# Heads and the turn of h ahead of a round of scores, and turned scores ahead of the queries

## The reference

```python
q, k, v = x @ wq.T, x @ wk.T, x @ wv.T            # 16 heads of q, 4 of k and v
attn = softmax(where(causal, q @ k / sqrt(16), -inf))
h = c + (attn @ v) @ wo.T
w, sel = top_k(rmsnorm(h) @ gate_w.T, 2)
```

## Time and profile before

| | us |
|---|---|
| median of 3 runs | 2118.55 |
| lowest, highest | 2116.47, 2120.29 |
| profiled execution | 2111.37 |
| its span | 2109.7 |
| TensorE busy | 2036.1 (97%) |
| VectorE busy | 1347.3 (64%) |
| ScalarE busy | 1117.4 (53%) |
| GpSimd busy | 963.0 (46%) |

### The profile page before, as it was taken

The page is one execution under the profiler, slowest core; times in us unless marked ns, Lnnn a source line. Parts: engine busy times, 40 slices in busy tenths (PEclk is TensorE's granted clock), DMA queues, the critical chain, the costliest instruction groups (busy, mean ns, idle before and its releaser), DMA issues. The chain is left out here.

```text
span 2109.7 us, 50236 instructions
## 1 busy us (share of the span) xinstructions
PE 2036.1 (97%) x17544; PEld 1752.2 (83%) x17544; DVE 1347.3 (64%) x2818; ACT 1117.4 (53%) x2219; POOL 963.0 (46%) x1062
## 2 busy tenths in 40 slices
PE   7999989999999999989979999999899999999997
PEld 7999985666666666659979999999888888888886
DVE  7888954676777767765636776788654444444452
ACT  6777744666666666655543333344354444454542
POOL 0000002365565556556644444444245656565653
PEclk9999987999999999989989999999999999999998
DMA  8767711133233232229864444544344444545442
GB/s 294 264 260 267 261 59 31 62 104 96 92 108 110 87 106 96 78 92 305 300 218 144 148 151 142 175 150 151 104 96 109 95 111 95 112 96 111 96 83 30
DMA packets 134682, 289.62 MB, mean 137 GB/s; under 512 B 23026, under 2 KB 64755, under 8 KB 128243
## 3 DMA queue, kind: packets, MB, share of 16 engines
q1 hardware_dynamic: 84466, 177.25, 24.9%
q0 software_dynamic: 50048, 110.14, 20.3%
HBM read 187.17 MB, written 95.42 MB: 134 GB/s over the span
## 5 line engine op out<-in xcount | busy, mean ns | idle before, releaser
L1248 DVE TENSOR_REDUCE neg_max<-ring 128x2 f32<-128x512 f32 (+1 forms) x384 | 250.0, 681 | 106.4 <-PE ring L1734 106.1
L1041 POOL TENSOR_SCALAR_AFFINE_SELECT weights_diag<-weights_diag 128x512 f32<-128x512 f32 x256 | 158.3, 643 | 258.4 <-ACT weights_diag L1139 258.1
L2908 POOL DMA_INDIRECT out<-q_t,row_put x128 | 201.8, 1576 | 162.4 <-ACT q_t L2972 137.7
L3046 DVE TENSOR_TENSOR ex_hid<-ex_up_ps,gelu 128x512 f32<-128x512 f32 x128 | 86.9, 688 | 171.8 <-ACT gelu L2956 171.8
L2956 ACT ACTIVATE gelu<-ex_gate_ps 128x512 f32<-128x512 f32 x128 | 76.3, 596 | 187.3 <-PE ex_up_ps L62 187.3
L2379 POOL DMA_INDIRECT picked_rows<-results,lo_row_now x128 | 134.0, 1047 | 56.3 <-issue 29.8
L1139 ACT ACTIVATE weights_diag<-ring 128x512 f32<-128x512 f32 x256 | 138.5, 599 | 24.2 <-PE ring L1752 24.2
L60 PE MATMUL ex_down_ps<-ex_dn_lo,ex_hid_hi 128*128 128x256 f32 x512 | 145.1, 283 | 2.8 <-issue 2.8
L61 PE MATMUL ex_down_ps<-ex_dn_hi,ex_hid_lo 128*128 128x256 f32 x512 | 145.2, 284 | 0.0
L62 PE MATMUL ex_down_ps<-ex_dn_hi,ex_hid_hi 128*128 128x256 f32 x512 | 144.9, 283 | 0.0
L1049 POOL DMA_INDIRECT sorted_rows<-h_sb,row_now x128 | 126.8, 990 | 34.8 <-issue 31.3
(11 more groups left out here) (404 smaller groups left out, 7521.8 us busy)
## 6 DMA issues: line engine op xcount, KB each, us to landing
ug_raw<-in_w_ug SPq DMA_DIRECT2D x32, 1028.0 KB, 5.0
dn_raw<-in_w_dn SPq DMA_DIRECT2D x32, 640.0 KB, 5.2
q_t<-sorted_rows SPq DMA_DIRECT2D x136, 128.0 KB
moe_w<-in_expert_gu SPq DMA_DIRECT2D x16, 1024.0 KB, 4.8
results<-c0n POOLq DMA_DIRECT2D x33, 256.0 KB, 4.4
x_raw<-in_x_t SPq DMA_DIRECT2D x32, 256.0 KB, 5.1
c0n<-c SPq DMA_DIRECT2D x32, 256.0 KB, 4.3
c0r<-c SPq DMA_DIRECT2D x32, 256.0 KB
```

The lines of the kernel that those rows point to most:

```text
L1041: nc.gpsimd.affine_select(part, part, [[0, G], [1, P]], ALU.is_ge, 0.0, base=0, channel_multiplier=-1).then_inc(kept_done, 1)
L1248: nc.vector.tensor_reduce(out, src, AX_X, ALU.max, negate=True).then_inc(max_done, 1)
L2908: nc.gpsimd.indirect_dma_start(out=out_rows, out_offset=bass.IndirectOffsetOnAxis(ap=at, axis=0), in_=eo[c][:, n, :], in_offset=None, comp ...
L3046: nc.vector.tensor_tensor(hid[f % 2][:], up_ps[f % 2][:], gelu[f % 2][:], ALU.mult).then_inc(hid_done, 1)
```

## The change

TensorE: heads q0 comes ahead of the turn of h, heads q1 ahead of S1, and T2 ahead of the first half of the queries. VectorE: the first maximum of S1 comes behind the reciprocal and the quotients of q1. ScalarE: the third and fourth exponent of T0 come ahead of the square sums of batch i+3, and those behind `norm_high`. No instruction is added or removed, and no wait is: each waits for what it waited for before, in its new place.

```diff
@@ ScalarE, body(i)
                 if has:
                     exps(i, 0, (0, 1))
-                if exists(later(i, 3)):
-                    front.square_sums(act, i[1] + 3)
-                if has:
                     exps(i, 0, (2, 3))
                 if has_next:
                     front.norm_high(act, i[1] + 2)
+                if exists(later(i, 3)):
+                    front.square_sums(act, i[1] + 3)
                 if has_before:
                     empty_values(i, 1)
@@ VectorE, body(i)
                     divide(i, 0)
                 if has_h:
                     h_low(i)
-                if has_scores:
-                    maxima(s, 1, 0)
                 if has_before:
                     inverse_sums(i, 1)
                 if picks:
...
                 if has_before:
                     divide(i, 1)
                 if has_scores:
+                    maxima(s, 1, 0)
                     maxima(s, 1, 1)
@@ TensorE, body(i)
                 if has:
                     turned_scores(i, 1)
+                if has_before:
+                    heads(i, 0)
                 if has_h:
                     turn_h(i)
                 if has_before:
-                    heads(i, 0)
+                    heads(i, 1)
                 if has_scores:
                     scores(i, 1)
-                if has_before:
-                    heads(i, 1)
                 if has_next:
                     keys_values(i)
-                    queries(i, 0)
                 if has:
                     turned_scores(i, 2)
+                if has_next:
+                    queries(i, 0)
```

## The result

| | before | after |
|---|---|---|
| median of the comparison | 2119.26 | **2136.30** |
| lowest, highest (4 runs each) | 2116.47, 2120.29 | 2132.94, 2138.62 |
| ratio, 95% interval | | 1.0081, 1.0063 to 1.0100 |
| profiled execution | 2111.37 | 2138.62 |
| its span | 2109.7 | 2137.0 |

The change costs 17 us, 0.8%; forecast were 21.4 us and 2140. The profiled spans differ by more, 27.3 us, since the profiled execution of before was 5 us under its fastest timed one, and that of after was its slowest. By the starts of T0 the 27.3 us split as follows: up to step 2 -3.5; steps 2 to 29 +20.0 (544.66 to 564.66); step 30 +1.6; from T0 of step 31 through layer 0's experts +3.9, and through the next stage +5.3. Apart from step 31 the last two lie outside the edits. TensorE spent 28.6 instead of 14.2 us of the one, and 15.8 instead of 10.5 of the other, at a granted clock of 0.5.

The account below looks back on a forecast made before the run. TensorE, busy for 97% of the span, was taken as the bound. 16 batches x 0.47 = 7.5, 13 x 0.97 = 12.6 and ends +1.3 gave +21.4 us on 2118.55, so 2140 us; range 2129 to 2149.

Parts of the forecast that it names:

- T2's wait: In batches with picks, T2 waits for S1's maxima behind a late `chosen`: +0.50 us in each of thirteen.
- Heads q1 waits for VectorE: Heads q1, now ahead of S1, waits 0.53 us for VectorE's quotients: +0.58 us per batch.
- S1's hidden wait: Inside S1, key groups 2 and 3 wait for T1's exponents; starting later removes this: -0.19 us per batch.
- Switches around T2: T2 ahead of the queries changes passes to row-tiled products: 0 to 0.1 us, taken as +0.08 per batch.
- ScalarE's copy taken at nothing: Values copy ahead of heads q0: square sums of 0.96 us fit in its 1.36 us of waiting, costing nothing.
- rival 1: `chosen` slips in between two of GpSimd's selects and T2 is not held up: 2133.5 us; chance 0.22.
- Ends: First and last batches: batch 30 +1.5 us, batch 31 -0.2, batches -1 and 0 nothing; together +1.3 us.
- rival 2: Two idle gaps in each even batch halve TensorE's clock: 32 us on top, 2172 us; chance 0.07.

Follow-up runs that it names:

- e12: The changed kernel a third time, nothing altered, timed beside the kernel before: 2122.59 us, ratio 1.0047.
- e1: The kernel before with only the heads order of TensorE and VectorE changed: 2128.75 us, ratio 1.0075.
- e7: The changed kernel with the turn of h ahead of both heads rounds: 2136.37 us, ratio 1.0100 to the kernel before.
- e2: The kernel before with only T2 put ahead of the first half of the queries: 2123.62 us, ratio 1.0040.
- e10: The kernel before with T2 ahead of the first queries everywhere and `chosen` moved behind S1's second maximum: 2112.82 us, ratio 0.9990.
- e5: The kernel before with the changed heads order and T2 ahead of the first queries, ScalarE's order as before: 2126.92 us, ratio 1.0055.
- e3: The kernel before with only ScalarE's order changed: 2111.37 us, ratio 0.9994.
- e8: The changed kernel once more, nothing altered, timed beside the kernel before: 2124.15 us, ratio 1.0045.
- e4: The changed kernel with heads q1 back behind S1 and VectorE's first maximum back ahead of q1's reciprocal: 2117.13 us, ratio 1.0012 to the kernel before.
- e9: The kernel before with T2 ahead of the first queries only in steps without picks: 2107.70 us, ratio 0.9972.
- e11: The kernel of e10 with ScalarE's order changed too: 2110.84 us, ratio 0.9980 to the kernel before.

## Why the prediction was right, and where it was not

The number was near, 2140 against 2136.3, and inside the range. That is in part luck. The mechanism behind most of it was right, but one term (T2's wait, 6.5 us) did not occur, the start of the stage gained what I had put at nothing, and an execution with late counts, which I had not forecast, filled the gap. In the two other comparisons the same change cost less than half of the forecast.

- **Heads q1 waits for VectorE: right.** In e12 heads q1 starts 665.93 - 663.39 = 2.54 us after T1, and the forecast was 664.45 - 661.91 = 2.54. The waits show it about once in each step, e1 has it alone, e7 lengthens the step by 0.44, which is what the turn covered.
- **S1's hidden wait goes: right**, 1.35 us. Together with the wait I had 0.39 us a step; e1 measured 0.45 and 0.47. What the other 0.06 to 0.08 are stays open.
- **Switches around T2, +0.08: wrong in sign in odd steps.** e2 has -0.07 there. In even ones the kernels with the new place take 0.04 to 0.05 more (e10, e5); what of this is the place is not shown. As a sum over the steps that is about -0.5 us instead of +2.3.
- **ScalarE's copy taken at nothing: right** by e3, e8 and e12. Late copies there were in the first comparison, but ScalarE was idle before them in all steps but step 10. There the square sums did hold the copy, once late high parts had used up the cover.
- **T2 held up in even steps, +0.50 each, 6.5 us: wrong.** The step that failed is "So I take that `chosen` ends at 647.52 as before". It ended at the next joint of two selects, and rival 1 describes that: no T2 waits for the maxima in steps 4 to 28 of e12 or of the changed kernel. The row for `gap` misled me, and it was not the nearest: in each trace `gap` took 1.55 us in step 30 alone and 0.10 to 0.16 in all others. For `chosen` the rows of before said as much: it started at 646.90, at the joint of the third and fourth select (645.09 + 1.79 = 646.88), so its 0.62 us were one select as well. In step 26 of before it came just at that joint and took 0.13. The rule of the Trainium skill (SBUF — State Buffer, section "Who interferes with whom"), by which the one that starts first keeps the ports for its whole instruction, was the better guide: `chosen` waited for one instruction at most in all these traces (0.61, 0.32). `gap`, at 1.55 us through two joints, does not fit it in the traces of before and after.
- **Ends, +1.3: near for step 30, but blind to the start.** Step 30 took 1.6 us more in two of the three traces of the change and 2.5 in e12 (forecast +1.5). I had counted batches -1 and 0 at nothing. With T2 ahead, step 0 takes 24.0 to 24.6 us, and without it 25.2 to 26.3, in all traces. In e8 T0 of step 2 comes at 359.0 instead of 363.3, so -4.3 us, at less half clock. Of these 3.3 lie ahead of step 0. T0 of step 0 starts at 314.6 to 315.8 in seven of the eight traces with ScalarE's new order (317.8 in e7) and at 317.1 to 318.4 in the six without it. So that order probably gives some 3 us at the start; in e3, which has it alone, longer steps 0 and 1 took most of that back.
- **The clock, rival 2:** no half clock in the middle of the stage in the change, with a gap of some 0.4 us in every step. Such stretches came in e2 and e4, where T2 waits, but in e10 too, where nothing does; so what decides them stays open.

The sum for e8, by its trace: -4.3 before step 2, +12.75 in steps 2 to 29, +1.6 in step 30, -0.8 behind it, 9.2 us (spans 2118.9 and 2109.7). That is the price of the change in two of three comparisons, and my 21.4 are more than twice that. Rival 1's 14.9 us come closer: its 0.47 in each of 28 steps are 13.2, against 12.75. In the first comparison the same kernel had the late counts on top. Its span is 18.1 us above that of e8, and 564.66 - 557.41 = 7.3 of these lie between steps 2 and 30. Another 4.1 and 5.9 lie in the two stretches behind, with 14.6 and 5.7 us more at half clock. So late copies can account for the 7.3 and not for the whole. That all four executions of the first comparison were disturbed alike is what their times suggest; only one was profiled.

Open is why TensorE's counts came late in that execution. ScalarE's order, the heads order and T2's place, alone or in the pairs tried, don't bring it, nor does the whole kernel in e8 and e12, and it reaches into a stage where nothing was changed. So it most likely belongs to the execution or to its chip, and which of them is not shown: e8 and e12 ran on two different chips, and which one ran the first comparison isn't on record.

## What to carry to other kernels

Before two rounds are put next to each other that use one bank in turn, take the other engine's answer from the trace. Here it is 0.80 us, and it begins only 0.17 after TensorE could go on (0.66 against 0.49). Subtract what stands between (0.44): the remaining wait of 0.53, less what the move frees (0.19 in S1), is paid in every step, however small the move looks. When a tiny operation takes long, look for rows of that very operation before borrowing another's: here `chosen` had its own. A reordering is worth splitting into its parts on the chip: here one part cost 0.45 us a step, and one gave 0.07 in half of the steps and lost 0.38 in the others. Confined to the first half (e9), that one came with a faster kernel. And where a difference is below 1%, compare a second time before explaining it: the same kernel came out 17, 10 and 9 us behind.

## What the runs showed of the hardware

- TensorE's semaphore counts can come late while its next matmuls start on time: in one execution the copies behind them started 0.4 to 0.6 us late in 21 of 25 steps (1.1 in two more, in one of them with the square sums' part), and counts were late in the next stage too. In two other executions of the same kernel none was in these stretches.
- The clock fell to half for 6.8 us in the middle of the stage in e10, with TensorE busy for 10.00 of the 10 us before, at a place where e11, the same on TensorE, kept it. The five such stretches in the middle of the stage (two in e2, two in e4, one in e10) cost 3.1 us each. In the stage behind the experts of layer 0, where no kernel differs, 10.1 to 22.4 us ran at 1.2 GHz.
- A VectorE operation between GpSimd's back-to-back selects got in at the next joint (`chosen`, 0.32 to 0.62 us in the rows shown), but one (`gap`, 1.55 us in step 30) missed two.
